# A two-layer transformer with routed experts: indirect stores, expert weights and one sequence's gathers at other places of a written-out order

## The chip, the core and the metric

The kernel runs on one core of a Trainium2 chip. The metric is the device time of one execution in microseconds (us). Engines: TensorE (PE, matrix products), VectorE (DVE), ScalarE (ACT), GpSimd (POOL) and SyncE (SP, which only issues DMAs). Each engine runs its own list of instructions in order and waits on semaphores for the others. All DMAs that SP issues stand in one queue, spread over the core's 16 DMA engines; indirect DMAs are issued from POOL and have a queue of their own.

## What is computed

Sixteen sequences of 512 tokens with 256 channels pass four blocks with residuals; each begins with a layer norm.

```
x = x + attention(norm(x))      # 16 heads of 16, rotary, window of 128 keys
x = x + experts(norm(x))        # router picks 2 of 8 experts for each token
x = x + attention(norm(x))      # 16 heads, xpos rotary, biases, full causal
x = x + norm(x) @ ternary(w).T  # weights rounded to -1, 0, 1 times a scale
```

An expert is `y = (silu(x W1a + b) * (x W1b + b)) W2 + b2` with a hidden width of 512. A token's two results are added with the softmax weights of the two experts, scaled to sum to one.

## The kernel before

The program has three phases. Phase one (tensors a0, attention and router together, from 0 to about 1100 us) and phase three (a1, attention and ternary product, from about 1807 us) are built by one function, `pipeline`. Phase two, `experts`, lies between them.

**The written-out order.** `pipeline` works in turns `i` = -2 to 17. In turn `i` several sequences are in flight, each at another stage: sequence `m = i + 2` is normed, projected to queries and keys, rotated and split into bf16 parts; sequence `s = i + 1` has its scores computed once (steps S) so that DVE finds each row's maximum; sequence `i` has its scores computed transposed (steps T), exponentiated on ACT and multiplied by the values (PV); sequence `o = i - 1` gets its output product, second norm and, in phase one, its router scores ("gates", 20 steps on DVE); the normed rows of sequence `r = i - 2` are stored by expert. `turn(i)` gives each step a number between about 0 and 1, its place in the turn. The steps are sorted by that number, and every engine takes from the sorted list those that concern it, in that order. The numbers thus set the order on each engine, not a time; semaphores do the waiting.

**The loop that passes through DRAM.** The parts of queries and keys of sequence `m` go PE (L994) -> DVE rotation (L871 in phase one, L867 in phase three) -> POOL (L526, L527 combine; L533, L537 take the parts apart, with ACT casts L601 and L604 between) -> SP stores to `a_parts_dram` (L434, nine DMAs) -> SP loads them back by head, `a_qst` and `a_kst`, one pair for each of four head groups ("stack", L444). Head group 3's pair has the place 1.0, the end of the turn. The negated row maxima (`a_nmt`, 16 KB, L449) of the sequence that is next are stored between the stacks of groups 1 and 2; the first T product (L1122) of the next turn waits for them.

**Scatters.** The eight steps ("scatter", r, k) of a turn are indirect DMAs (L507) that POOL issues: two choices of expert times four blocks of 128 tokens. Besides its rows, a scatter waits until the stack of head group 3 of the sequence `r + 3` has landed, and until ACT has done the exponentials that stand ahead of it in the order (`exps_before`).

**Expert weights.** The 24 chunks of the experts' weights (8 experts, 3 each, 128 x 1024 floats) are split in phase one into a high part and a remainder: "fetch" (SP, L408, 512 KB in), "high" (ACT, L556), "rest" (POOL, L476, the subtraction) and "keep" (SP, L413, 1024 KB out to `ws_dram`). There is one buffer: a fetch waits until the chunk before has been kept. A table, `CHUNKS`, says in which turn and where each begins: two in turn -1, one in each of turns 0 to 13, four in each of turns 14 and 15.

**Second fill.** Phase three begins by loading two rows per token from the experts' output `ys`, with indirect DMAs on POOL ("gather", L517), and DVE adds them with their weights ("mix", L725). Turns -2 and -1 fill the pipeline. DVE's mixes of a sequence wait for its gathers; sequence 1's stood in turn -2 behind all that POOL does for sequence 0's queries and keys. At the start of turn -1 stands "quantise" (DVE L680 to L695, PE L1011), the rounding of the last weights, and PE takes v of sequence 0 (L994) and its S steps behind it.

Of the kernel before, what the change touches and what calls it, by code (L numbers as in the profile page):

```python
# [26 lines left out]
NE, FF = 8, 512  # L27
# [78 lines left out]
def pipeline(nc, name, x_in, x_out, w_all, w_out, tables, biases, window, scale, consts, routed, mixed, ternary_w):  # L106
# [22 lines left out]
    def main_steps(i):  # L129

        units = [(g, b) for g in range(NG) for b in range(NT)]
        t_of = {b: [k for k, st in enumerate(t_steps) if st[0] == b] for b in range(NT)}

        def scores(u):
            return [(t_steps[k][2] * t_steps[k][4] + 256, ("T", i, u[0], k)) for k in t_of[u[1]]]

        timed = scores(units[0])
        for n, u in enumerate(units):
            nxt = scores(units[n + 1]) if n + 1 < len(units) else []
            timed += nxt[:1] + [(4 * p_width[u[1]], ("PV", i) + u)] + nxt[1:]  # L140
        total, at, out = sum(c for c, _ in timed), 0, []
        for c, st in timed:
            out.append(((at + c / 2) / total, st))
            at += c
        return out

    def turn(i):
        s, m, o = i + 1, i + 2, i - 1
        out = []
        if 0 <= i < B:  # L150
            out += [(0.05, ("minus", i, 1, 0)), (0.19, ("minus", i, 1, 1))]
            main = main_steps(i)
            out += main
            done = {st[2]: pos for pos, st in main if st[0] == "PV" and st[3] == NT - 1}
            for g in range(NG):
                out.append((done[g] + 0.001, ("sums", i, g)))
                if g < NG - 1:
                    out += [(done[g] + 0.035, ("flip", i, g)), (done[g] + 0.055, ("scale", i, g))]
        if 0 <= o < B:
            out += [(0.02, ("flip", o, NG - 1)), (0.04, ("scale", o, NG - 1)), (0.08, ("back", o, 0)),  # L160
                    (0.105, ("back", o, 1)), (0.13, ("out", o, 0)), (0.15, ("out", o, 1)), (0.155, ("add", o, 0)),
                    (0.175, ("add", o, 1))]
            out += [(0.185 + 0.015 * t, ("stats2", o, t)) for t in range(NT)] + [(0.235, ("aggr2", o))]
            if routed:
                out += [(0.28 + 0.02 * t, ("norm2", o, t)) for t in range(NT)]
                out += [(0.18, ("y", o)), (0.54, ("turn2", o, 0)), (0.56, ("turn2", o, 1)), (0.64, ("score", o)),
                        (0.789, ("exp2", o)), (0.873, ("place", o))]
                out += [(0.76 + 0.0112 * k, ("gates", o, k)) for k in range(20)]
            else:
                out += [(0.255 + 0.015 * t, ("norm2", o, t)) for t in range(NT)]  # L170
                out += [(0.355, ("turn2", o, 0)), (0.37, ("turn2", o, 1)), (0.41, ("last", o, 0)), (0.42, ("last", o, 1)),
                        (0.435, ("final", o, 0)), (0.445, ("final", o, 1)), (0.45, ("y", o))]
        if routed and 0 <= i - 2 < B:
            out += [(0.165 + 0.024 * k, ("scatter", i - 2, k)) for k in range(2 * NT)]
        if routed:
            for j, (at_turn, at) in enumerate(CHUNKS):
                if at_turn == i:
                    out += [(at, ("fetch", j)), (at + 0.14, ("high", j)), (at + 0.145, ("rest", j)), (at + 0.17, ("keep", j))]
            if i == B:
                out.append((0.03, ("pads",)))  # L180
        if 0 <= s < B:
            lo, hi = 0.03, 0.97
            out += [(lo + (hi - lo) * (k + 0.5) / NS, ("S", s, k // NSG, k % NSG)) for k in range(NS)]
            out += [(0.01, ("v", s)), (0.035, ("vcopy", s, 0)), (0.055, ("vcopy", s, 1)), (0.575 if mixed else 0.70, ("minus", s, 0, 0)), (0.68 if mixed else 0.78, ("minus", s, 0, 1))]
        for n, back in ((m, 1), (m + 1, 0)):
            if not 0 <= n < B or n == m and m and not mixed:
                continue
            if mixed:
                steps = [(0.48, ("load", n)), (1.07, ("aggr", n))]
                for t in range(NT):  # L190
                    first = 0.69 + 0.01 * t if n == 1 else 0.36 + 0.02 * t
                    steps += [(first, ("gather", n, 0, t)), (0.775 + 0.03 * t, ("mix", n, 0, t)),
                              (0.80 + 0.03 * t if n else 0.44 + 0.02 * t, ("gather", n, 1, t)), (0.92 + 0.022 * t, ("mix", n, 1, t)),
                              (1.0 + 0.015 * t, ("stats", n, t))]
            else:
                steps = [(0.55, ("load", n)), (0.88, ("aggr", n))] + [(0.80 + 0.02 * t, ("stats", n, t)) for t in range(NT)]
            out += [(at - back, st) for at, st in steps if n == 0 and back or n and int(at) == back]
        if biases and 0 <= m < B:
            out.append((0.26 if m else 0.99, ("shift", m)))
        if biases and m == 0:  # L200
# [22 lines left out]
    with ctx:  # L223
        def sb(n, shape, dt=F32):
            return ctx.enter_context(nc.sbuf_tensor(f"{name}_{n}", shape, dt))
# [32 lines left out]
        stats, stats2 = (sb(f"stats{i}", [P, NT, 6]) for i in range(2))  # L258
# [916 lines left out]
NW = KC * 2 * FF + FC * D  # L1175
WCOLS = 2 * FF


CHUNKS = [(-1, 0.25), (-1, 0.60)] + [(i, 0.13) for i in range(B - 2)] \
    + [(i, 0.02 + 0.18 * n) for i in (B - 2, B - 1) for n in range(4)]  # L1180


def turns_of_two(fori, step, count):

    step(None, Seq(None, 0))
# [378 lines left out]
```

How the kernel before makes its waits and increments, by code:

```python
        @block.sync  # L389
        def _(sp):
            if mixed:
                sp.dma_start(yrow[:, :, :], yrow_d).then_inc(index_loaded, 16)
                sp.dma_start(gate[:, :, :], gate_d).then_inc(index_loaded, 16)
            sp.dma_start(xt[0][:, :, :], x_in[0].rearrange("(t p) d -> p t d", p=P)).then_inc(x_loaded[0], 16)
            sp.dma_start(w_raw, w_all).then_inc(w_loaded, 16)
            sp.dma_start(ident[:, :], ident_d).then_inc(ident_loaded, 16)
            for dst, src in loads:
                sp.dma_start(dst, src).then_inc(const_loaded, 16)
            sp.wait_ge(ones_done, 1)
            for i in range(2):
                sp.dma_start(kst[i][ROWS:AUG, :, :], junk[0:2 * H, 0, :]).then_inc(ones_loaded, 16)
            for st in order:
                if st[0] == "fetch":
                    j = st[1]
                    e, c = divmod(j, NW // WCOLS)
                    src = w1_d[e][:, c, :] if c < KC else w2_d[e].rearrange("p c n -> p (c n)")
                    sp.wait_ge(ws_stored, 16 * j)
                    sp.dma_start(ws[:, 1, :], src).then_inc(ws_loaded, 16)
                elif st[0] == "keep":
                    j = st[1]
                    e, c = divmod(j, NW // WCOLS)
                    sp.wait_ge(rest_done, j + 1)
                    sp.dma_start(ws_d[e][:, :, c * WCOLS:(c + 1) * WCOLS], ws[:, :, :]).then_inc(ws_stored, 16)
                elif st[0] == "pads":
                    sp.wait_ge(counted_rows, 1)
```

## Time and profile before

| | us |
|---|---|
| median of three runs (2976.92 to 2982.33) | 2978.64 |
| the profiled execution, its own time | 2977.46 |
| its span, first to last instruction | 2975.8 |
| PE busy | 2530.3 (85%) |
| DVE busy | 1704.9 (57%) |
| ACT busy | 1375.7 (46%) |
| POOL busy | 922.9 (31%) |

The mean granted clock of TensorE was 0.927 of full speed. Read the busy shares as averages over three phases. The order is fixed, so a wait of one engine is handed on to all that stand behind it in the order of another. The chain of waits of the whole program says little of phase one, since it ends where the second phase's loops begin; the turns of phase one are read with sums by stretch, the waits of single turns, and the engines' instructions in order of time. A turn is counted here from one first exponential (ACT L629) of a sequence to that of the next.

### The profile page before, as it was taken

The page shows a single profiled execution, that of the slowest core. Times are in us where ns is not written, and L with a number is a line of the kernel's source. Part 1 is how long each engine was busy: PE and PEld are TensorE (multiplying, and loading weights), DVE is VectorE, ACT ScalarE, POOL GpSimd, SP SyncE. Part 2 cuts the span into 40 slices and gives each one's busy share as a digit, 9 for nine tenths or more (in the row PEclk, how much of TensorE's full clock was granted, in tenths as well). Part 3 has the DMA queues.
Part 4 walks back from the last instruction along what each step waited for, and adds up shares of the span by engine and source line. Part 5 has one row for each costly group of instructions (what it writes and reads, how often), then busy time and mean ns, then how long its engine had stood idle before and what let it go on. Part 6 is the DMA issues. An engine that isn't in the chain of part 4 may idle for free. (4 is left out here: it accounts for less than half of the span.)

```text
span 2975.8 us, 51500 instructions
## 1 busy us (share of the span) xinstructions
PE 2530.3 (85%) x17918; PEld 1733.0 (58%) x17918; DVE 1704.9 (57%) x5704; ACT 1375.7 (46%) x2419; POOL 922.9 (31%) x863
## 2 busy tenths in 40 slices
PE   3688888888888739999999993489989999999897
PEld 2355555555565428888888882245555555555554
DVE  3566666666766334444444442576667776666751
ACT  2345555555555413333333331156555655565553
POOL 3424553345435220000000003443444443344300
PEclk7799999999999759999999996699999999999998
DMA  4555556555665367767767753454344445344420
GB/s 136 182 168 166 160 160 184 172 157 155 184 174 169 139 227 250 252 239 253 260 238 251 258 206 106 127 166 126 114 120 143 134 142 145 115 114 135 122 72 15
DMA packets 261846, 493.73 MB, mean 166 GB/s; under 512 B 25608, under 2 KB 192904, under 8 KB 251656
## 3 DMA queue, kind: packets, MB, share of 16 engines
q1 hardware_dynamic: 243736, 437.07, 47.2%
q0 software_dynamic: 17904, 54.02, 5.4%
q8 instruction: 117, 1.92, 0.3%
q14 instruction: 89, 0.73, 0.1%
HBM read 301.48 MB, written 188.35 MB: 165 GB/s over the span
## 5 line engine op out<-in xcount | busy, mean ns | idle before, releaser
L629 ACT ACTIVATE a_pr<-a_bank 128x512 f32<-128x512 f32 (+1 forms) x1152 | 641.6, 573 | 559.9 <-PE a_bank L999 546.0
L887 DVE CUSTOM_DVE_ANT_0 a_junk<-a_bank,a_smask 128x256 bf16<-128x256 f32 (+3 forms) x1536 | 654.7, 464 | 405.4 <-PE a_bank L1096 404.2
L1096 PE MATMUL a_bank<-a_kst,a_qst 96*128 96x256 bf16 (+3 forms) x2048 | 452.4, 295 | 81.1 <-DVE a_nmax L887 29.1
L1122 PE MATMUL a_bank<-a_qst,a_kst 98*128 98x256 bf16 (+3 forms) x2048 | 442.6, 291 | 44.5 <-ACT a_pr L629 27.1
L1140 PE MATMUL a_bank<-a_pr,a_va 128*32 128x256 f32 (+3 forms) x4096 | 358.1, 426 | 83.0 <-ACT a_pr L629 80.0
L1401 PE MATMUL e_bank<-e_xh,e_w 128*128 128x512 f32 x1248 | 391.0, 395 | 1.4 <-DVE e_xl L1382 1.4
L1096 PEld LDWEIGHTS a_bank<-a_kst,a_qst 96*128 96x128 bf16 x2048 | 171.8, 101 | 329.9 <-DVE a_nmax L887 95.2
L999 PE MATMUL a_bank<-a_mask,a_identb 128*128 128x512 bf16 (+2 forms) x1152 | 359.8, 312 | 0.0
L1122 PEld LDWEIGHTS a_bank<-a_qst,a_kst 98*128 98x128 bf16 x2048 | 182.6, 102 | 163.6 <-ACT a_pr L629 75.0
L1401 PEld LDWEIGHTS e_bank<-e_xh,e_w 128*128 128x128 f32 x1248 | 229.6, 189 | 48.7 <-DVE e_xl L1382 1.8
L1401 PE MATMUL e_bank<-e_xl,e_w 128*128 128x512 f32 x624 | 246.5, 395 | 0.0
L1345 ACT ACTIVATE e_sa<-e_bank,e_b 128x512 f32<-128x512 f32 x156 | 107.3, 688 | 289.3 <-PE e_bank L1401 289.2
L1323 POOL DMA_DIRECT2D ys<-e_yt x39 | 29.5, 756 | 677.2 <-DVE e_yt L1363 659.8
L1374 DVE SCALAR_TENSOR_TENSOR e_gf<-e_bank,e_b,e_sa 128x512 f32<-128x512 f32 x156 | 117.2, 751 | 194.5 <-ACT e_sa L1345 194.5
L1415 PE MATMUL e_bank<-e_w,e_gh 128*128 128x256 f32 x1248 | 221.0, 278 | 2.9 <-DVE e_gl L1378 2.9
L1140 PEld LDWEIGHTS a_bank<-a_pr,a_va 128*32 128x32 f32 x4096 | 86.0, 111 | 225.0 <-issue 115.9
L507 POOL DMA_INDIRECT xs<-e_rn,e_row x128 | 127.7, 998 | 234.0 <-DMA a_kst<-a_parts_dram 127.9
L1415 PEld LDWEIGHTS e_bank<-e_w,e_gh 128*128 128x128 f32 x1248 | 192.3, 189 | 4.8 <-DVE e_gl L1378 3.4
L882 DVE TENSOR_REDUCE a_nmax<-a_bank 128x2 f32<-128x512 f32 (+1 forms) x192 | 130.1, 685 | 83.1 <-PE a_bank L999 83.1
L1415 PE MATMUL e_bank<-e_w,e_gl 128*128 128x256 f32 x624 | 173.3, 278 | 0.0
L1378 DVE TENSOR_TENSOR e_gl<-e_gf,e_gh 128x512 fp32r<-128x512 f32 x156 | 108.0, 693 | 109.8 <-ACT e_gh L1350 109.8
L1350 ACT CAST e_gh<-e_gf 128x512 fp32r<-128x512 f32 x156 | 96.9, 621 | 143.2 <-DVE e_gf L1374 143.2
(173 smaller groups left out, 4545.2 us busy)
## 6 DMA issues: line engine op xcount, KB each, us to landing
e_w<-ws_dram SPq DMA_DIRECT2D x39, 2048.0 KB, 8.8
a_parts_dram<-a_parts SPq DMA_DIRECT2D x224, 256.0 KB, 3.9
a_qst<-a_parts_dram SPq DMA_DIRECT2D x128, 384.0 KB, 7.0
a_kst<-a_parts_dram SPq DMA_DIRECT2D x128, 384.0 KB, 8.6
e_w<-ws_dram SPq DMA_DIRECT2D x39, 1024.0 KB, 6.0
a_parts_dram<-a_parts SPq DMA_DIRECT2D x32, 768.0 KB, 3.7
ws_dram<-a_ws SPq DMA_DIRECT2D x24, 1024.0 KB, 4.4
e_xg<-xs SPq DMA_DIRECT2D x39, 512.0 KB, 6.5
```

The source lines that it names most:

```text
L507: pool.indirect_dma_start(xs, bass.IndirectOffsetOnAxis(ap=row[r % 2][:, k, t:t + 1], axis=0), rn[r % 2][:, t, :], None).then_inc(scattere ...
L629: nc.scalar.activation(pr[b][:, h:h + per, :], TB_[at % 2][:, 0:per * w].rearrange("p (h w) -> p h w", h=per), ACT.Exp, scale=scale).then_ ...
L882: last = nc.vector.tensor_reduce(nmax[:, qb, g * HG + h:g * HG + h + per], SB_[at % 2][:, 0:per * w].rearrange("p (h w) -> p h w", h=per), ...
L887: last = nc.vector.tensor_tensor_reduce(junk[:, at % 2, j * w:(j + 1) * w], SB_[at % 2][:, j * w:(j + 1) * w], smask[:, T - w:T], scale=-1 ...
L999: return nc.tensor.matmul(out, identb[:, :], rhs, start=False, stop=True, skip_group_check=True)
L1096: last = nc.tensor.matmul(out[:, j * w:(j + 1) * w], q[0:ROWS, hh, qb * P:(qb + 1) * P], k[0:ROWS, hh, k0:k0 + w], start=not whole or j == ...
L1122: nc.tensor.matmul(out[:, j * w:(j + 1) * w], k[0:AUG, hh, b * P:(b + 1) * P], q[0:AUG, hh, q0:q0 + w], start=(j == 0), stop=False, skip_g ...
L1140: last = nc.tensor.matmul(PVB[32 * j:32 * (j + 1), q0:q0 + w], va[i % 2][:, b, (g * HG + j) * VW:(g * HG + j) * VW + 32], pr[b][:, j, :], ...
L1374: nc.vector.scalar_tensor_tensor(gf[f % 2][:, :], BB[f % 2][:, :], b1[s.slot][:, FC + f:FC + f + 1], sa[f % 2][:, :], ALU.add, ALU.mult).t ...
L1378: nc.vector.tensor_tensor(gl[s.slot][:, f, :], gf[f % 2][:, :], gh[s.slot][:, f, :].bitcast(F32), ALU.subtract).then_inc(gl_done, 1)
L1401: last = nc.tensor.matmul(out[:, :], first(s.slot, low)[:, kc, col:col + P], x[s.slot][:, kc, :], start=(p == 0), stop=(p == 3 * KC - 1))
L1415: last = nc.tensor.matmul(YB[n][:, (t % 2) * D:(t % 2 + 1) * D], x[s.slot][:, f, t * P:(t + 1) * P], second(s.slot, low)[:, f, :], start=( ...
```

## The change

Four edits, all but one of them numbers of the table of places.

1. The eight scatters of a turn stand at 0.135 + 0.018 k, before at 0.165 + 0.024 k.
2. The router's steps on DVE: the first fifteen gates at 0.73 to 0.877 (before 0.76 to 0.917), the last five at 0.92 to 0.968 (before 0.928 to 0.973); "exp2" at 0.757 (0.789), PE's "place" at 0.90 (0.873).
3. Chunks: two in each of turns 0 to 11, at 0.13 and 0.62; none in turns -1 and 12 to 15. The high part is still cast on ACT, the remainder is still taken on POOL.
4. Phase three, sequence 1 alone: its load, gathers, mixes and statistics stand in turn -2 among the projection steps of sequence 0, before between places 0.48 of turn -2 and 0.07 of turn -1.

```diff
-                        (0.789, ("exp2", o)), (0.873, ("place", o))]
-                out += [(0.76 + 0.0112 * k, ("gates", o, k)) for k in range(20)]
+                        (0.757, ("exp2", o)), (0.90, ("place", o))]
+                out += [(0.73 + 0.0105 * k if k < 15 else 0.92 + 0.012 * (k - 15), ("gates", o, k)) for k in range(20)]
...
-            out += [(0.165 + 0.024 * k, ("scatter", i - 2, k)) for k in range(2 * NT)]
+            out += [(0.135 + 0.018 * k, ("scatter", i - 2, k)) for k in range(2 * NT)]
...
-            for j, (at_turn, at) in enumerate(CHUNKS):
-                if at_turn == i:
-                    out += [(at, ("fetch", j)), (at + 0.14, ("high", j)), (at + 0.145, ("rest", j)), (at + 0.17, ("keep", j))]
+            for j, (fetch, high, rest, keep) in ((2 * i, (0.13, 0.27, 0.275, 0.29)), (2 * i + 1, (0.62, 0.90, 0.915, 0.93))):
+                if 0 <= j < NE * NW // WCOLS:
+                    out += [(fetch, ("fetch", j)), (high, ("high", j)), (rest, ("rest", j)), (keep, ("keep", j))]
...
-                steps = [(0.48, ("load", n)), (1.07, ("aggr", n))]
+                steps = [(0.48, ("load", n)), (1.07, ("aggr", n))] if n != 1 else [(-0.30, ("load", n)), (0.295, ("aggr", n))]
                 for t in range(NT):
-                    first = 0.69 + 0.01 * t if n == 1 else 0.36 + 0.02 * t
+                    if n == 1:
+                        steps += [(0.002 + 0.005 * t, ("gather", n, 0, t)), (0.075 + 0.01 * t, ("mix", n, 0, t)),
...
```

**POOL, one turn of the middle of phase one.** `xs<-e_rn,e_row` are scatters, `a_lean1` and its like the second norm's statistics (aggr2), `a_ws` the remainder of a chunk, `a_qk<-a_rt` the rotation of the new sequence. Before:

```order
L507 DMA xs<-e_rn,e_row 69632x256 x3
L493 TENSOR_SCALAR a_lean<-a_mv 128x4
L494 TENSOR_SCALAR a_ve<-a_mv 128x4
L496 TENSOR_TENSOR a_rstd<-a_ve,a_power 128x4
L498 TENSOR_TENSOR a_shift<-a_lean,a_rstd 128x4
L507 DMA xs<-e_rn,e_row 69632x256 x2
L476 TENSOR_TENSOR a_ws<-a_ws 128x1024
L507 DMA xs<-e_rn,e_row 69632x256 x3
L526 TENSOR_TENSOR a_qk<-a_rt 128x512
```

The same stretch now, from the end of the turn before (L481 is now the line of the remainder, L512 of the scatters):

```order
L481 TENSOR_TENSOR a_ws<-a_ws 128x1024
L512 DMA xs<-e_rn,e_row 69632x256 x6
L498 TENSOR_SCALAR a_lean<-a_mv 128x4
L499 TENSOR_SCALAR a_ve<-a_mv 128x4
L501 TENSOR_TENSOR a_rstd<-a_ve,a_power 128x4
L503 TENSOR_TENSOR a_shift<-a_lean,a_rstd 128x4
L512 DMA xs<-e_rn,e_row 69632x256 x2
L481 TENSOR_TENSOR a_ws<-a_ws 128x1024
L531 TENSOR_TENSOR a_qk<-a_rt 128x512
```

Six scatters instead of three stand ahead of the second norm's statistics, and all eight ahead of the first chunk's remainder. What stands ahead of the rotation in the turn is the same in sum; the second chunk's remainder is new and stands at the end of the turn before.

**SP, from the load of a sequence to the start of the next turn.** `a_qst` and `a_kst` of 96x2048 are the stacks of one head group, `a_qst<-a_nmt` the row maxima. Before:

```order
L426 DMA a_xt<-in_x 128x4x256
L434 DMA a_parts_dram<-a_parts 128x2x512 x6
L444 DMA a_qst<-a_parts_dram 96x2048
L444 DMA a_kst<-a_parts_dram 96x2048
L444 DMA a_qst<-a_parts_dram 96x2048
L444 DMA a_kst<-a_parts_dram 96x2048
L449 DMA a_qst<-a_nmt 2x8x512
L444 DMA a_qst<-a_parts_dram 96x2048
L444 DMA a_kst<-a_parts_dram 96x2048
L444 DMA a_qst<-a_parts_dram 96x2048
L444 DMA a_kst<-a_parts_dram 96x2048
L408 DMA a_ws<-in_we 128x1024
```

Now, the same stretch up to the stack of group 3, without its first two pairs' rows:

```order
L431 DMA a_xt<-in_x 128x4x256
L413 DMA a_ws<-in_we 128x1024
L439 DMA a_parts_dram<-a_parts 128x2x512 x6
```

```order
L454 DMA a_qst<-a_nmt 2x8x512
L449 DMA a_qst<-a_parts_dram 96x2048
L449 DMA a_kst<-a_parts_dram 96x2048
L418 DMA ws_dram<-a_ws 256x1x1024
L449 DMA a_qst<-a_parts_dram 96x2048
L449 DMA a_kst<-a_parts_dram 96x2048
L413 DMA a_ws<-in_we 128x1024
```

The second chunk's fetch (512 KB) stands ahead of the six stores, and its keep (1024 KB) ahead of head group 3's stack.

**DVE, second fill (phase three, turn -2 into -1).** `a_xt<-a_yg` are mixes; L680 and what follows is the rounding of the weights. Before:

```order
L853 TENSOR_TENSOR a_xl<-a_bank,a_xh 128x512
L867 SCALAR_TENSOR_TENSOR a_rt<-a_bank,a_bqk,a_tab 128x512 x8
L725 SCALAR_TENSOR_TENSOR a_xt<-a_yg,a_gate,a_xt 128x256 x8
L703 BN_STATS a_stats<-a_xt 128x6
L680 MEMSET a_ot 128x128
L681 TENSOR_REDUCE a_mv<-a_on 128x1
```

Now:

```order
L730 SCALAR_TENSOR_TENSOR a_xt<-a_yg,a_gate,a_xt 128x256 x4
L858 TENSOR_TENSOR a_xl<-a_bank,a_xh 128x512
L679 COPY a_ot<-a_ot 128x127 x2
L682 TENSOR_TENSOR a_boa<-a_bank,a_ot 128x256
L858 TENSOR_TENSOR a_xl<-a_bank,a_xh 128x512
L730 SCALAR_TENSOR_TENSOR a_xt<-a_yg,a_gate,a_xt 128x256 x4
L708 BN_STATS a_stats<-a_xt 128x6 x4
L714 BN_AGGR a_mv<-a_stats 128x2 x4
L872 SCALAR_TENSOR_TENSOR a_rt<-a_bank,a_bqk,a_tab 128x512 x8
L685 MEMSET a_ot 128x128
L686 TENSOR_REDUCE a_mv<-a_on 128x1
```

The eight mixes of sequence 1 stood between the rotations and the rounding; four now stand ahead of sequence 0's turning, four between its projections' inputs and its rotations.

## Rows read from the trace of the kernel before

**Rows 1.** Sums by stretch, turns of phase one: us, then busy us by engine
```profile
50.00:109.70 59.70, 28.69 (x129) 17.18 (x130) 30.23 (x148) 8.51 (x12) 19.74 (x14) 0.64 0.71 207
164.30:223.10 58.80, 52.88 (x428) 34.24 (x428) 40.40 (x198) 32.18 (x57) 19.22 (x17) 0.92 0.51 152
223.10:823.20 600.10, 523.15 (x4262) 342.22 (x4261) 397.34 (x1980) 321.88 (x561) 272.53 (x250) 0.93 0.55 168
823.20:940.80 117.60, 102.84 (x855) 67.92 (x854) 78.17 (x388) 64.26 (x113) 52.80 (x46) 0.94 0.55 167
940.80:1001.90 61.10, 50.06 (x370) 28.89 (x368) 32.93 (x180) 28.23 (x49) 18.97 (x16) 0.80 0.46 156
1001.90:1053.50 51.60, 39.20 (x291) 21.23 (x291) 11.53 (x48) 25.68 (x46) 18.98 (x16) 0.80 0.40 143
```
**Rows 2.** Instructions in order of time, PE, turn 5: start, us, [idle before]
```profile
433.24 1.08 PE L1140 MATMUL a_bank<-a_pr,a_va 128*32 128x256 f32 x8 [3.95 <-ACT a_pr L629]
...
452.82 0.18 PE L1046 MATMUL a_bank<-a_chosen,a_before 128*128 128x8 bf16 x1 [2.10 <-DVE a_chosen L783]
...
462.19 0.39 PE L1122 MATMUL a_bank<-a_qst,a_kst 98*128 98x256 bf16 x2 [0.71 <-DMA a_qst<-a_nmt]
```
**Rows 3.** Sums by stretch, the 3.4 us behind the first of these stalls
```profile
433.30:436.70 3.40, 3.40 (x26) 1.40 (x27) 2.37 (x10) 2.13 (x4) 3.34 (x3) 0.50 0.00 0
```
**Rows 4.** Instructions in order of time, POOL and DVE, turn 5
```profile
409.13 1.10 POOL L507 DMA_INDIRECT xs<-e_rn,e_row  x1 [11.13 <-DMA a_kst<-a_parts_dram]
...
424.15 1.28 DVE L871 TENSOR_TENSOR a_rt<-a_bank,a_tab 128x512 f32<-128x512 f32 x2
...
429.13 1.27 POOL L526 TENSOR_TENSOR a_qk<-a_rt 128x512 f32<-128x512 f32 x1
```
**Rows 5.** Instructions in order of time, POOL, turn 1, which has no scatters
```profile
188.31 1.29 POOL L526 TENSOR_TENSOR a_qk<-a_rt 128x512 f32<-128x512 f32 x1 [3.08 <-DVE a_rt L871]
```
**Rows 6.** DMA issues in order of time, SP, turn 5
```profile
444.97 4.22 SPq L434 DMA_DIRECT2D a_parts_dram<-a_parts  x6
...
453.77 0.42 SPq L444 DMA_DIRECT2D a_kst<-a_parts_dram  x1
```
**Rows 7.** DMA issues in order of time, SP, turn -1, which has two chunks
```profile
87.07 4.65 SPq L434 DMA_DIRECT2D a_parts_dram<-a_parts  x6
...
97.25 0.43 SPq L444 DMA_DIRECT2D a_kst<-a_parts_dram  x1
97.72 0.56 SPq L413 DMA_DIRECT2D ws_dram<-a_ws  x1
```
**Rows 8.** DMA issues by line, 97.2 to 97.9 us: KB, us from issue to landing
```profile
ws_dram<-a_ws SPq DMA_DIRECT2D x1, 1024.0 KB, 7.1
...
a_kst<-a_parts_dram SPq DMA_DIRECT2D x1, 384.0 KB, 4.9
```
**Rows 9.** Instructions in order of time, PE, end of turn -1
```profile
108.58 0.61 PE L1122 MATMUL a_bank<-a_qst,a_kst 98*128 98x256 bf16 x2 [8.44 <-DMA a_qst<-a_nmt]
```
**Rows 10.** Who waited for whom, 940.8 to 1001.9 us, turn 14: us, times, longest
```profile
PE a_bank L1140 <- ACT a_pr L629: 8.9, 3, 3.3
ACT a_ws L556 <- DMA a_ws<-in_we: 8.6, 3, 3.6
```
**Rows 11.** Who waited for whom, 1001.9 to 1053.5 us, turn 15
```profile
PE a_bank L1140 <- ACT a_pr L629: 11.2, 5, 4.3
```
**Rows 12.** Instructions in order of time, all engines, the second fill
```profile
1815.29 1.76 DVE L668 TENSOR_TENSOR a_wl<-a_rt,a_wh 128x1536 fp32r<-128x1536 f32 x1 [7.49 <-ACT a_wh L551]
1815.62 2.25 POOL L517 DMA_INDIRECT a_xn<-ys,a_yrow  x1 [0.30 <-issue]
...
1874.39 0.35 SPq L444 DMA_DIRECT2D a_qst<-a_parts_dram  x1
...
1886.76 0.59 PE L1011 MATMUL a_bank<-a_mv,a_ot 128*128 128x1 f32 x2 [36.90 <-DVE a_mv L681]
...
1891.73 0.40 PE L1096 MATMUL a_bank<-a_kst,a_qst 96*128 96x128 bf16 x4
```

More of the change, by code:

```diff
@@ L188, in turn @@
             if mixed:
-                steps = [(0.48, ("load", n)), (1.07, ("aggr", n))]
+                steps = [(0.48, ("load", n)), (1.07, ("aggr", n))] if n != 1 else [(-0.30, ("load", n)), (0.295, ("aggr", n))]
                 for t in range(NT):
-                    first = 0.69 + 0.01 * t if n == 1 else 0.36 + 0.02 * t
+                    if n == 1:
+                        steps += [(0.002 + 0.005 * t, ("gather", n, 0, t)), (0.075 + 0.01 * t, ("mix", n, 0, t)),
+                                  (0.08 + 0.01 * t, ("gather", n, 1, t)), (0.23 + 0.01 * t, ("mix", n, 1, t)),
+                                  (0.275 + 0.005 * t, ("stats", n, t))]
+                        continue
+                    first = 0.36 + 0.02 * t
                     steps += [(first, ("gather", n, 0, t)), (0.775 + 0.03 * t, ("mix", n, 0, t)),
@@ L196, in turn @@
                 steps = [(0.55, ("load", n)), (0.88, ("aggr", n))] + [(0.80 + 0.02 * t, ("stats", n, t)) for t in range(NT)]
-            out += [(at - back, st) for at, st in steps if n == 0 and back or n and int(at) == back]
+            out += [(at - back, st) for at, st in steps if n == 0 and back or n and (at >= 1) == back]
         if biases and 0 <= m < B:
@@ L1176 @@
 WCOLS = 2 * FF
-CHUNKS = [(-1, 0.25), (-1, 0.60)] + [(i, 0.13) for i in range(B - 2)] \
-    + [(i, 0.02 + 0.18 * n) for i in (B - 2, B - 1) for n in range(4)]
 def turns_of_two(fori, step, count):
```

## The prediction, made before the changed kernel had run

> **What bounds the kernel now.** The sums by stretch come first [rows 1]: from turn 2 on a turn of phase one takes 60.0 us (600.1 for ten), PE is busy for 52.3 of them, DVE 39.7, ACT 32.2, POOL 27.3, and the DMA engines 55%. Turn 1, which has no scatters yet, takes 58.8. So PE leads, but 7.7 us of a turn it stands still. PE's instructions in order of time show where [rows 2]: 3.95 us for an exponential, 2.10 for the router's choice on DVE, 0.71 for the landing of the row maxima at the first T product of the next turn. The 3.4 us behind such a stall are at the lower clock level, 1.2 GHz instead of 2.4 [rows 3], so each stall costs some 1.7 us more.
>
> It would be wrong to add all this up as gain, because the last of the three waits ends a loop through DRAM that is as long as the turn. From the first exponential of turn 5 (402.7) the loop runs: rotation inputs ready on DVE 425.4, that is 22.7 us later; POOL begins the rotation at 429.1, 3.7 us late, since scatters and a chunk's remainder are ahead of it [rows 4]; six stores from 445.0, 15.8 us later; the pair of stacks at 453.8 [rows 6], 8.8 later; first T product at 462.2 [rows 2], 8.4 later. 22.7 + 3.7 + 15.8 + 8.8 + 8.4 = 59.4, and 0.65 to the exponential is 60.1, the turn. PE waits only 0.71 us at the end because its own stalls fill the time. What is taken from PE's stalls alone comes back as a longer wait at L1122. I read the change by this loop.
>
> **Turns 2 to 11: scatters, gates and a second chunk.**
> - The scatters begin when the stack of head group 3 has landed, at 409.1 [rows 4]. From there to the rotation POOL spends 20.0 us, some of it waiting for exponentials between scatters. At the closer places all eight need only T steps that are done by then, so this wait goes; work of about 15 us is left (eight issues of 1.1 with 0.2 to 0.3 between, 2.5 for the statistics, 2.4 for the remainder), and the rotation could start at once when its inputs are there: 3.7 us gained, no more.
> - The second chunk's keep now stands ahead of head group 3's stack. In turn -1 a keep stood so: a stack landed at 97.25 + 4.9 = 102.2, the keep behind it at 97.72 + 7.1 = 104.8 [rows 7, 8]. It takes 2.6 us of the queue, and the scatters begin so much later, at about 411.7: with 15 us of work the rotation would start at 426.8, 1.4 late instead of 3.7. So 2.3 gained.
> - The second fetch stands ahead of the six stores. Turn -1 again shows it: first store to the stack of keys took 97.25 - 87.07 = 10.2 us there [rows 7], 8.8 in turn 5 [rows 6]. 1.4 lost.
> - PE's stalls at L1140 and L1046 shrink or go (place is later by 0.027, the choice earlier by 0.034 of a turn, 3.7 us together, against a wait of 2.10), but the loop ends when it ends, so PE waits some 5 us at L1122 instead, and what follows runs at the lower clock. This lengthens the beginning of the loop: in turn 1, which begins so, the inputs come at 188.3 [rows 5], 24.0 us after its exponential at 164.3 [rows 1], against 22.7: 1.3 lost.
> - Second "high" on ACT and "rest" on POOL (2.4 us): ACT waits for PE at the end of a turn, POOL is idle there. Nothing, as long as the remainder is done before the queue has worked off the stacks of groups 0 to 2. Should it not be, its 2.4 us delay the scatters too.
>
> Sum: -2.3 + 1.4 + 1.3 = +0.4; with rounding I take 0 per turn, 0 for ten. Bounds per turn: -3.7 (no loss from the DMAs) to +4.0 (keep and fetch both in full on the loop, 2.6 + 1.4), that is -37 to +40.
>
> **Turns 0 and 1**: the fetch's 1.4 each, nothing to gain: +2.8. **Turns 12 and 13** lose their one chunk: now 117.6 for two [rows 1]; without remainder and with early scatters they follow turn 1: -1.8.
>
> **Turn -1** loses two chunks. At its end PE waits 8.44 us for the row maxima until 108.58 [rows 9]. Fetch and keep are in the queue ahead of them: 1.4 and 2.6 as above, and about 0.3 for what the first chunk's remainder costs POOL. -4.3; bounds 0 and -8.4, the whole wait.
>
> **Turns 14 and 15** lose eight chunks, and here lies most of the gain, since no loop through DRAM is left (no new sequence is projected). Turn 14 takes 61.1 us with fewer products than the turns before; the clock is at 0.80 of full, against 0.93 [rows 1]. ACT stands three times for a fetch, 8.6 us, and PE for its exponentials 8.9 [rows 10]; in turn 15 PE stands 11.2 [rows 11]. With four chunks through one buffer, each cast waits for its load. Turn 14: of PE's 8.9 some 3 stay, because the second norm waits for POOL's six scatters ahead of its statistics; 5.9 go, with 1.6 at L1046. A clock of 0.80 means 40% of the time at the lower level: 24 us, in which 12 are lost; I give back 7.5, since a stall or two remain. -15.0; bounds -8.6 (ACT's own waits alone) and -22. Turn 15: 11.2 less the same 3 is 8.2; its 20 us at the lower level lose 10, of which I give back 5: -13; bounds -7 and -20. Behind turn 15 nothing is gained or lost: padding the expert regions begins when its gates are done and needs its time.
>
> **Second fill of phase three.** PE stands 36.9 us, to 1886.76, for the rounding on DVE, which stands behind sequence 1's mixes; v takes until 1891.73, where the S steps begin [rows 12]. In the new order the rounding follows the rotations directly, and v is long done. The next to end is then the stack of sequence 0: issued at 1874.39 [rows 12], its key half takes 4.9 us where nothing crowds it [rows 8], so 1879.3 to 1879.7. That is -12.2. Sequence 0's own path: DVE and POOL wait for each other and for gathers there, so four gathers and four mixes before its norm are hidden; I take 0.2 lost. **A rule that speaks against this:** one gather took 2.25 us, twice the 1.1 of a scatter's issue [rows 4, 12], while DVE ran the 1.76 us of L668 beside it [rows 12]. The Trainium skill (SBUF — State Buffer, section "SBUF: two separate sides") says that GpSimd can't write a DMA's descriptors while VectorE holds the port pair both share. By it the moved gathers, now beside DVE's mixes, could each take up to 1.1 us longer, four of them ahead of sequence 0's statistics: the fill would give -8 instead of -12. L668 moves six times as many elements as a mix, so I expect less. Bounds: -6 and -14.
>
> **Sum.** 0 + 2.8 - 1.8 - 4.3 - 15.0 - 13.0 - 12.0 = -43.3. Against the profiled execution's own time (2977.5; its span is 1.7 shorter) 2934.2; the median lies 1.2 above that execution: 2935.4, I say 2936.
>
> **Rivals.**
> - *The loop doesn't bind.* If the maxima come early once stores and stacks are issued earlier, each of turns 2 to 13 gets the 3.7 us: another -40, 2895. For it: POOL, which starts the loop, gets freer. Against: turn 1, with the rotation on time, is only 1.2 shorter and ends in the same DMA wait.
> - *The queue binds (the other side).* Keep, fetch and stacks of a turn share one queue; if the keep lengthens the loop too, by a later start of POOL, and the six scatters ahead of the second norm hold ACT and so the T products, a turn grows by 2.6 + 1.4 + 1.4 = 5.4, twelve turns by 65: 2936 + 65 = 3001. It decides from 3.6 us per turn on. For it: DMA is busy 55% and crowded just there. Against: the keep stands behind the maxima in the queue.
> - *The last turns give back little.* With exponentials and T products taking turns on two banks, the stalls of turns 14 and 15 stay in other places, and the clock low: only the 8.6 and 7 of the fetch waits go, 12 less gain: 2948.
> - *Nothing in sum.* Turns grow by 3 to 4 us and eat the rest: 2977.
>
> **How the numbers follow.** My forecast 0.60, its own range 2920 to 2951; the last turns give back little 0.17; the loop doesn't bind 0.09; the queue binds 0.10 (0.08 of it slower); nothing in sum 0.04. A measurement of this kernel tells 0.2%, 6 us, from no change. Slower 0.08, same 0.04, faster 0.88. The range, 2908 to 2962, takes in the two inner cases and half of each outer one.
>
> **What would show it.** Right: turns 2 to 11 at 59 to 61.5 us, POOL's rotation no longer 3.7 us late, the wait at L1046 gone, and instead 3 to 7 us of PE at the first T product for the row maxima; the scatters beginning about 2.6 us later after that product's turn start; turn 14 at 44 to 49 us and turn 15 at 36 to 41, with a clock above 0.85; the first T product of turn 0 near 104; S steps of the second fill from about 1880 less the gain before. Wrong: turns 2 to 11 beyond 62 or under 58, ACT waiting at the second norm for 5 us and more, or a second fill whose first S product waits for DVE again.

## The result, and where the time went

The changed kernel takes 2932.82 us (median of four runs; one of them, at 3707.74 us, was disturbed and is left out of the ratio). The kernel before, run with it, takes 2980.48. The ratio is 0.9834, 95% interval 0.9814 to 0.9855: by the ratio 49 us less, where 43 were forecast. The profiled execution took 2926.71 us, its span is 2925.0 at a mean granted clock of 0.943 (0.927 before). The line numbers of the engines' parts of `pipeline` are larger by five in the changed kernel: L629 is now L634, L1122 is L1127.

The sums by stretch of the changed kernel, which answer to [rows 1] (turn -1, turn 1, turns 2 to 11, 12 and 13, 14, 15):

```profile
50.00:104.40 54.40, 28.15 (x128) 17.02 (x130) 30.22 (x148) 6.91 (x11) 15.12 (x12) 0.66 0.62 169
161.70:221.40 59.70, 51.49 (x422) 33.89 (x428) 41.49 (x198) 32.81 (x58) 21.56 (x18) 0.95 0.56 176
221.40:822.00 600.60, 510.10 (x4192) 337.04 (x4261) 412.72 (x1980) 327.73 (x571) 295.85 (x260) 0.96 0.62 194
822.00:936.30 114.30, 101.51 (x840) 66.90 (x853) 79.08 (x388) 61.60 (x110) 48.00 (x44) 0.97 0.50 152
936.30:982.30 46.00, 40.49 (x364) 24.67 (x368) 31.53 (x175) 24.15 (x45) 9.56 (x12) 0.96 0.19 58
982.30:1023.60 41.30, 33.93 (x286) 18.95 (x291) 12.99 (x60) 21.68 (x42) 9.53 (x12) 0.92 0.11 39
```

The ten steady turns together did not move (600.1 to 600.6 us), although POOL has 23 us more to do in them. Turn 14 lost 15.1 us, turn 15 10.3, and the clock of both rose from 0.80 to 0.96 and 0.92.

PE's waits in the ten turns tell how that zero came about. First the kernel before (223.1 to 823.2 us), then the changed one (221.4 to 822.0); columns: who waited for whom, us in total, times, longest:

```profile
PE a_bank L1140 <- ACT a_pr L629: 39.7, 10, 4.0
PE a_bank L1046 <- DVE a_chosen L783: 21.1, 10, 2.1
...
PE a_bank L1122 <- DMA a_qst<-a_nmt: 2.2, 3, 0.8
```
```profile
PE a_bank L1127 <- DMA a_qst<-a_nmt: 28.5, 10, 4.7
PE a_bank L1101 <- DVE a_nmax L892: 21.2, 28, 1.0
PE a_bank L1153 <- ACT a_nmt L625: 10.3, 10, 1.1
...
PE a_bank L1145 <- ACT a_pr L634: 7.4, 13, 1.0
```

The two big stalls, 61 us in ten turns, are gone but for 7.4 us in pieces of 1.0 at most. In their place PE waits 28.5 us for the row maxima at the first T product, 21 for DVE's maxima in short pieces, 10 for the copy of the maxima.

The larger of the two old stalls, at the exponentials, had not begun with PE. In turn 5 of the kernel before, ACT stood for POOL's rotation ahead of the exponentials that PE waited for until 433.24 [rows 2]:

```profile
431.65 1.05 ACT L601 CAST a_parts<-a_qk 128x1024 bf16<-128x1024 f32 x1 [6.90 <-POOL a_qk L527]
432.60 1.08 ACT L629 ACTIVATE a_pr<-a_bank 128x512 f32<-128x512 f32 x2
```

POOL's late rotation thus stands behind this stall as well as in the loop through the stores. In the ten turns ACT waited 69.1 us for it before and 36.8 us in the changed kernel.

Turn 5 of the changed kernel, engine by engine:

```profile
408.66 1.10 POOL L512 DMA_INDIRECT xs<-e_rn,e_row  x1 [12.77 <-DMA a_kst<-a_parts_dram]
...
423.38 1.29 POOL L531 TENSOR_TENSOR a_qk<-a_rt 128x512 f32<-128x512 f32 x1
```
```profile
421.53 1.28 DVE L876 TENSOR_TENSOR a_rt<-a_bank,a_tab 128x512 f32<-128x512 f32 x2
```
```profile
439.55 4.27 SPq L439 DMA_DIRECT2D a_parts_dram<-a_parts  x6
...
450.04 0.42 SPq L449 DMA_DIRECT2D a_kst<-a_parts_dram  x1
...
451.45 0.67 SPq L454 DMA_DIRECT2D a_qst<-a_nmt  x1
```
```profile
458.15 0.39 PE L1127 MATMUL a_bank<-a_qst,a_kst 98*128 98x256 bf16 x2 [1.96 <-DMA a_qst<-a_nmt]
```

The turn began at 400.12. POOL now begins the rotation 23.3 us into it, 0.6 us behind DVE's last input (422.8); in [rows 4] it was 26.4 and 3.7 us late. From there to the stores it takes 16.2 us (15.8 before). From the stores to the stack of keys it takes 10.5 where [rows 6] had 8.8.

**The second fill.** PE's first S product of phase three, which came behind DVE's rounding in [rows 12]:

```profile
1848.82 0.61 PE L1101 MATMUL a_bank<-a_kst,a_qst 96*128 96x128 bf16 x4 [18.96 <-DMA a_kst<-a_parts_dram]
```

It comes 71.8 us after DVE's first instruction of the phase (1777.05); before, 84.4 (1807.32 to 1891.73). It waits for the stack, no longer for DVE.

### The profile page after: what moved, and what is told of

It reads as the page before. It is cut to its first block and busy times, and to the rows that moved or that the text cites. A ratio compares the mean times of both kernels' runs of the same rounds, so it can differ in the third digit from the quotient of the medians.

```text
span 2925.0 us, 51326 instructions
## 1 busy us (share of the span) xinstructions
PE 2492.1 (85%) x17745; PEld 1718.6 (59%) x17918; DVE 1723.0 (59%) x5704; ACT 1369.4 (47%) x2419; POOL 923.2 (32%) x863
## 5 line engine op out<-in xcount | busy, mean ns | idle before, releaser
L634 ACT ACTIVATE a_pr<-a_bank 128x512 f32<-128x512 f32 (+1 forms) x1152 | 638.0, 573 | 552.5 <-PE a_bank L1004 302.3
L1127 PE MATMUL a_bank<-a_qst,a_kst 98*128 98x256 bf16 (+3 forms) x2048 | 434.6, 286 | 72.9 <-DMA a_qst<-a_nmt 43.4
L1145 PE MATMUL a_bank<-a_pr,a_va 128*32 128x256 f32 (+3 forms) x4096 | 350.2, 418 | 35.5 <-ACT a_pr L634 33.8
L1127 PEld LDWEIGHTS a_bank<-a_qst,a_kst 98*128 98x128 bf16 x2048 | 178.3, 99 | 189.9 <-ACT a_pr L634 78.4
L1004 PE MATMUL a_bank<-a_mask,a_identb 128*128 128x128 bf16 (+2 forms) x979 | 283.3, 289 | 0.0
L512 POOL DMA_INDIRECT xs<-e_rn,e_row x128 | 127.7, 998 | 299.7 <-DMA a_kst<-a_parts_dram 138.2
```

The costliest lines, as they stand in the source:

```text
L512: pool.indirect_dma_start(xs, bass.IndirectOffsetOnAxis(ap=row[r % 2][:, k, t:t + 1], axis=0), rn[r % 2][:, t, :], None).then_inc(scattere ...
L634: nc.scalar.activation(pr[b][:, h:h + per, :], TB_[at % 2][:, 0:per * w].rearrange("p (h w) -> p h w", h=per), ACT.Exp, scale=scale).then_ ...
L1004: return nc.tensor.matmul(out, identb[:, :], rhs, start=False, stop=True, skip_group_check=True)
L1127: nc.tensor.matmul(out[:, j * w:(j + 1) * w], k[0:AUG, hh, b * P:(b + 1) * P], q[0:AUG, hh, q0:q0 + w], start=(j == 0), stop=False, skip_g ...
L1145: last = nc.tensor.matmul(PVB[32 * j:32 * (j + 1), q0:q0 + w], va[i % 2][:, b, (g * HG + j) * VW:(g * HG + j) * VW + 32], pr[b][:, j, :], ...
```

## The experiments

Two theories were to be told apart. **The loop**: a turn of phase one is as long as the way rotation - stores - stack - row maxima - first T product, and what PE's stalls give up comes back as a wait there. **The rivals**: PE's stalls bind, so the turn shrinks with them; or the queue binds, so it grows with every DMA put ahead. The table holds means over turns 2 to 11 of each kernel's one profile, in us after a turn's first exponential, worked out from the starts of the instructions in each trace.

```
                       first    rotation  six     stack    first T   next
                       scatter  on POOL   stores  of keys  product   turn
before                   6.5     26.4     42.7    50.5     59.4      60.0
changed                  8.8     24.0     40.4    50.6     59.3      60.1
chunks alone             8.4     26.7     43.2    52.7     61.6      62.2
scatters, gates alone    6.9     23.4     40.2    48.4     57.3      58.0
changed, fetch early     8.6     24.1     41.2    49.4     58.5      59.2
changed, keep behind     7.2     23.6     40.3    50.4     59.0      59.8
before, maxima first     7.1     26.4     42.8    50.7     58.9      59.5
changed, maxima first   11.1     25.9     43.4    53.6     59.8      60.5
 + keep behind           8.9     23.8     40.2    50.3     56.0      56.7
 + scatters' wait        6.6     22.8     39.4    49.6     55.4      56.1
```

How far one profile can be trusted shows where two kernels have the same order in these turns: the ten took 600.1 and 601.7 us (before; the fill alone), 600.6 and 604.2 (changed; with the late scatters of experiment 5), 560.9 and 572.6 (the last kernels of experiments 4 and 6). A difference under 0.4 us a turn is not shown by such a pair, and one of 1.2 came up once without a cause in the order.

**1. The three parts, each alone on the kernel before.** First the chunks, edit 3 of the change:

```diff
-            for j, (at_turn, at) in enumerate(CHUNKS):
+            for j, (fetch, high, rest, keep) in ((2 * i, (0.13, 0.27, 0.275, 0.29)), (2 * i + 1, (0.62, 0.90, 0.915, 0.93))):
```

> The kernel before with the chunks alone moved (two a turn in turns 0 to 11, none in -1 and 12 to 15). Scatters, gates and the second fill stay as they were. Loop theory: in turns 2 to 11 the keep delays the scatters by 2.6 us and the fetch the stores by 1.4, and nothing is won back, since the scatters keep their far places: up to +4.0 us a turn, so 62 to 64 us instead of 60.0. Against that turn -1 gives back some 5, turn 14 some 15, turn 15 some 10 us. Sum: +40 + 3 - 30 = about +10 us, 2988. Rival (the wider spacing hides the chunk, turns stay at 60): -30 us, 2950. Rival (the queue binds, 5.4 a turn): 3005.

2969.42 us, ratio 0.9973 (0.9961 to 0.9984). The turns 2 to 11 grew by 22.3 us, 2.2 each, and turns 14 and 15 lost 16.0 and 11.7. The direction in each place is the theory's; the cost per turn is half of the 4.0 that was the bound, so the sum has the other sign than expected.

Then the fill, edit 4:

```diff
-                steps = [(0.48, ("load", n)), (1.07, ("aggr", n))]
+                steps = [(0.48, ("load", n)), (1.07, ("aggr", n))] if n != 1 else [(-0.30, ("load", n)), (0.295, ("aggr", n))]
```

> The kernel before with the second fill alone changed. Theory A: all of the difference behind phase three's start belongs to this edit: 12.6 us until the first score product, some 4 in the rest of turn -1 and some 4.5 in the turns of phase three, so -21 us, 2959. Theory B: the 4 and the 4.5 are not this edit's but scatter of the execution: -12.6, 2968. Phase one and two unchanged within 1 us in both.

2963.59 us, ratio 0.9946 (0.9928 to 0.9964): -16 us, between the two. By the trace: first S product 13.2 us sooner (71.2 us after DVE's start against 84.4), from there to the first T product 45.4 against 48.2. All four profiles without this edit have 48.2 to 48.5, the ten with it 44.2 to 46.8. So 1.4 to 4 us in the rest of turn -1 are this edit's. A gain in the turns of phase three is not shown: they take 998.3 to 1002.6 us without the edit (1002.6 in the profile of before) and 996.6 to 1002.5 with it.

Last the scatters and gates, edits 1 and 2:

```diff
-            out += [(0.165 + 0.024 * k, ("scatter", i - 2, k)) for k in range(2 * NT)]
+            out += [(0.135 + 0.018 * k, ("scatter", i - 2, k)) for k in range(2 * NT)]
```

> The kernel before with scatters, gates, exp2 and place at the new places, chunks and fill as before. Loop theory: POOL begins the rotation on time (3.7 us earlier a turn), the turn's start runs slower by 1.3, so -2.4 us a turn in turns 2 to 13, about 57.7 instead of 60.0, -29 us in all, 2950; PE then waits for the row maxima instead of exponentials and the router's choice. Rival (PE's stalls bind, no loop): their 7.7 us a turn go, 52 to 54 us a turn, -75. Rival (POOL's delay did not matter): 60 us a turn, 2979.

2952.20 us, ratio 0.9918 (0.9886 to 0.9949). Turns 2 to 11 take 580.0 us, 2.0 less each, where the loop gave 2.4 and the rivals 7.7 or nothing. PE's stalls of 61 us went here too (4.2 are left), and 20 us came of it. The three parts' gains, 8.0 + 16.1 + 24.4 = 48.5 us by their ratios, make up the 49.5 of the whole, and in the ten turns +22.3 - 20.1 = +2.2 stands beside the +0.5 measured, which two profiles can't tell apart.

**2. The loop cut.** The row maxima of head half 0 stand in the order, and so in SP's queue, behind the stacks of groups 0 and 1. They were taken ahead of them, on SP alone:

```diff
-            for st in order:
+            ahead = [("minus", s, 0, 1) for s in range(B - 1)] if routed else []
+            for st in [early for st in order if st not in ahead
+                       for early in ([("minus", st[1] - 1, 0, 1)] if routed and st[0] == "stack" and st[1] and st[2] == 0 else []) + [st]]:
```

> The changed kernel, phase one alone edited: SP issues the row maxima's DMA (16 KB) of head half 0 ahead of the stacks of groups 0 and 1 instead of behind them. They are on the SBUF side ready at 442.3 in turn 5 and SP is free at 443.9, yet they are issued at 451.45. Loop theory: the first T product no longer waits for the loop (2.9 us a turn by the waits' sum); next is the stack of group 0, landed at 455, before PE's own work ends at 456.3. So -2 to -2.8 us a turn in 11 to 13 turns: -22 to -35 us, 2898 to 2911. Rival (another wait takes its place at once, such as the first S product for its stack, or DVE): 0 to -8 us. Slower would be a surprise.

2917.81 us, ratio 0.9802 (0.9782 to 0.9821), 9 us less than the changed kernel by the ratios, and the ten turns did not gain: 604.6 us. The wait for the maxima is gone from PE's list, the gain lies in turns -1 and 0 (the first exponential of turn 1 is at 148.8 instead of 161.7). The turn was bound by a second loop, which this profile shows, SP and POOL:

```profile
384.55 0.62 SPq L420 DMA_DIRECT2D ws_dram<-a_ws  x1
385.22 0.59 SPq L451 DMA_DIRECT2D a_qst<-a_parts_dram  x1
385.85 0.47 SPq L451 DMA_DIRECT2D a_kst<-a_parts_dram  x1
```
```profile
398.04 1.10 POOL L514 DMA_INDIRECT xs<-e_rn,e_row  x1 [13.51 <-DMA a_kst<-a_parts_dram]
```

The stack of head group 3, with the keep's 1024 KB just ahead, is issued at 385.85 in turn 4, and the first scatter, which waits for it, starts 12.2 us later; behind the scatters come the rotation (14.7 us), the six stores (17.4), the stack of keys (10.4), and again the stack of group 3 (5.8): 60.5 us, as long as the mean of the ten turns.

The same edit on the kernel before:

> The kernel before with the maxima's DMA alone ahead of the stacks of groups 0 and 1. PE waited only some 0.7 us a turn there. Theory (PE's own stalls at the exponentials and the router's choice, 6 us a turn, bind as long as the loop does): turns 2 to 11 gain no more than 1 us each, 59 to 60; turn -1 and turn 0 give 8 to 12 us as in the changed kernel; 2960 to 2970. Rival (the loop alone bound, the stalls only filled its time): turns 2 to 11 fall to 56 or 57, 2930 to 2940.

2955.87 us, ratio 0.9928 (0.9912 to 0.9945). The ten turns take 595.4 us, 0.5 less each, hardly more than two profiles differ by, and PE waits there as before:

```profile
PE a_bank L1142 <- ACT a_pr L631: 39.6, 10, 4.0
PE a_bank L1048 <- DVE a_chosen L785: 21.0, 10, 2.1
```

Of the 21 us gained, 10.0 lie ahead of turn 0 and 5.6 in turns 0 and 1. So in the kernel before two things were about equally long, the loop and PE's own work with its stalls. With the loop cut the stalls hold the turn (0.5 gained at most), and the larger of them is POOL's late rotation, for which ACT waits 69.1 us here too; with the stalls gone and POOL on time the loop holds it (2.0 gained, experiment 1).

**3. The terms of the queue, each alone on the changed kernel.** The second chunk's keep behind the stack of group 3:

```diff
-(2 * i + 1, (0.62, 0.90, 0.915, 0.93)))
+(2 * i + 1, (0.62, 0.90, 0.915, 1.001)))
```

> The changed kernel with only the second chunk's keep moved behind the stack of group 3. It measures the term of 2.6 us: scatters begin 8.5 us after a turn's first exponential now, and should begin 5 to 6 after it. Loop theory: the rotation begins up to 2 us earlier if its inputs are there, and the maxima's loop gets shorter by that: -0.5 to -2 us a turn in 11 turns, 2910 to 2925. Rival (the keep was free where it stood): 0, 2930. A loss of 1 to 2 us a turn if the fetch behind the keep now holds up the output and the second half of the maxima.

2930.79 us, ratio 0.9853 (0.9832 to 0.9874), no difference that can be told. The scatters begin 1.6 us earlier, the rotation only 0.3, since then it waits for its inputs; the turn shrinks by 0.3, which one profile doesn't show.

The second fetch at 0.31 instead of 0.62, out of the stores' way:

> The changed kernel with the second chunk's fetch alone moved from 0.62, ahead of the six stores, to 0.31, behind the first chunk's keep, where SP has nothing to do. It measures the term of 1.4 us. Theory (the fetch lengthens the maxima's loop): stores land 1.4 us earlier, turns 0 to 11 shorter by 0.7 to 1.4 us, 2916 to 2925. Rival (the fetch was free, or SP now waits for the keep's landing in front of the stores): 2930 or more, turns 2 to 11 at 60 us.

2925.29 us, ratio 0.9841 (0.9815 to 0.9866), which does not tell it from the changed kernel; the trace does. From the stores to the stack of keys it is 8.2 us instead of 10.2, but the stores are 0.8 later; the ten turns take 591.8 us, 0.9 less each, and PE's wait for the maxima falls from 28.5 to 10.3 us. As the queue stands here, the fetch is the larger of the two costs.

**4. Both loops cut.** Maxima first, and the keep at 1.001:

> The kernel with the maxima first, and the second chunk's keep at place 1.001, behind the stack of head group 3, instead of 0.93. Theory (two loops): with the maxima out of the way a second loop of 60.6 us bound the turn: in turn 5 of that kernel stack of group 3 issued 385.85, landed 398.04 (12.2 us, the keep's 1024 KB ahead of it), rotation 412.76 (14.7), stores 430.14 (17.4), stack of group 0 at 440.57 (10.4), the next at 446.41 (5.8). Without the keep ahead the stack of group 3 should land in some 7 us: the turn falls to 56 to 57.5 us, -3 to -4 in 11 to 12 turns: 2918 less 33 to 48, 2870 to 2885. Rival (the scatters, not the stack, are late): turns stay at 59 to 60, 2905 to 2918.

2880.73 us, ratio 0.9682 (0.9663 to 0.9701). The keep, worth 0.3 us a turn or nothing by itself, is worth 3.8 here: 566.5 us for ten turns against 604.6. Then, with these, the scatters wait for the stack of group 2:

```diff
-                        pool.wait_ge(stack_loaded[(r + 3) % 2][NG - 1], 32 * ((r + 3) // 2 + 1))
+                        pool.wait_ge(stack_loaded[(r + 3) % 2][NG - 2], 32 * ((r + 3) // 2 + 1))
```

> Maxima first, keep behind, and the scatters wait for the stack of head group 2 instead of 3. Theory: POOL starts the scatters some 5 us earlier, so the loop through stack 3, scatters and rotation is cut; then PE's own work and its short stalls bound the turn, 54.5 to 56.5 us, 2855 to 2875. Rival (scatters beside the stack slow both, or DVE and PE bind already): no more than 5 us below the kernel without this edit.

**2872.16 us, ratio 0.9642 (0.9623 to 0.9660): the best of all, 107 us below the kernel before and 57 below the changed one by the ratios.** Ten turns take 560.9 us:

```profile
208.10:769.00 560.90, 506.69 (x4263) 334.13 (x4262) 414.12 (x1980) 327.98 (x571) 295.93 (x260) 0.97 0.67 207
```

PE is busy for 50.7 of 56.1 us, and its list of waits holds no DMA.

**5. The last turns.** In the changed kernel PE still stood 3.18 us in turn 14 and 3.93 in turn 15, each for exponentials, while ACT waited for the second norm's statistics behind six scatters on POOL. First the changed kernel (936.3 to 1023.6 us), then the one of this experiment (940.2 to 1020.3):

```profile
ACT e_rn L583 <- POOL a_shift L503: 7.2, 2, 3.9
```
```profile
ACT e_rn L583 <- POOL a_shift L503: 2.9, 2, 1.9
```

The edit:

```diff
-            out += [(0.135 + 0.018 * k, ("scatter", i - 2, k)) for k in range(2 * NT)]
+            out += [((0.24 if i in (B - 2, B - 1) else 0.135) + 0.018 * k, ("scatter", i - 2, k)) for k in range(2 * NT)]
```

> The changed kernel with the scatters of turns 14 and 15 alone at 0.24 + 0.018 k, behind the second norm's statistics on POOL. It tests what is left of PE's stall there: 3.18 us at 951.38 and 3.93 at 996.79, each with a stretch at the lower clock. Theory (ACT's second norm waits for POOL's scatters): both gaps go, turn 14 from 46.0 to 42 to 43.5, turn 15 from 41.3 to 37 to 39, 2920 to 2926 in all. Rival (the scatters are late elsewhere and hold rn or the pads): turn 16 and what is behind it grows by the same, 2930.

2927.92 us, ratio 0.9837 (0.9820 to 0.9853); the total can't tell it, the two turns do:

```profile
940.20:983.60 43.40, 39.48 (x370) 24.16 (x368) 31.61 (x175) 24.09 (x46) 9.53 (x12) 1.00 0.21 63
983.60:1020.30 36.70, 32.21 (x291) 18.25 (x291) 12.94 (x58) 21.29 (x42) 9.53 (x12) 1.00 0.13 44
```

2.6 and 4.6 us less, and the granted clock 1.00 throughout. Nothing behind turn 15 got longer: from its end to DVE's first instruction of phase three it is 753.4 us in both.

**6. All together, which failed.** To the best kernel both the early fetch and the late scatters were added:

> All five together: maxima first, keep behind the stack of group 3, scatters waiting for group 2's stack, scatters of turns 14 and 15 behind the second norm's statistics, fetch at 0.31. If the last two add to the 2872 of the first three: turns 14 and 15 give 7 us; the fetch gives nothing once no loop binds (turns 2 to 11 stay at 56). 2863 to 2867. Rival (the loop through the stores still binds): turns at 55, 2850 to 2855.

2876.46 us, ratio 0.9667 (0.9651 to 0.9683), which doesn't tell it from the best kernel: not better. Then only the late scatters were added:

> Four of the five: maxima first, keep behind the stack of group 3, scatters waiting for group 2's stack, scatters of turns 14 and 15 late; the fetch back at 0.62. In the kernel with all five, turns 14 and 15 took 49.9 and 43.1 us, against 43.4 and 36.7 where the late scatters were tried alone, though the five kernels have the same order there. If the early fetch is what costs (by whatever it does to what lies before), turns 14 and 15 come to 43.4 and 36.7 here, 2863 to 2867. Rival (the late scatters cost once the turns before are shorter, or these two turns scatter from build to build): 47 to 50 and 41 to 43 again, 2873 to 2879.

2886.81 us, ratio 0.9689 (0.9665 to 0.9713), five runs from 2875.72 to 2894.49, slower than the best kernel. In both kernels turn 14 takes 49.9 and turn 15 43.1 us, instead of 43.4 and 36.7 (46.0 and 41.0 in the best kernel), so the fetch is not what costs. These two turns are only a part of what the last kernel lost: its ten turns take 572.6 us, against 560.9 and, with the early fetch, 560.3, though the late scatters change nothing there. Its profile is of the slowest of its five runs. Both have a wait like this in turn 15, here of the four edits:

```profile
971.48 0.90 PE L1155 MATMUL a_bank<-a_ident,a_ou 128*128 128x128 f32 x3 [4.40 <-ACT a_ou L645]
```

where in the kernel of experiment 5 the same step follows within a microsecond. The order of the instructions on ACT and DVE in these two turns is the same in all three kernels, and against experiment 5 both fall back in the same two short stretches, by about 6 us each: from 20 to 26 us into turn 14 and from 63 to 67. ACT stands at its copy (L645) 2.29 us for an event the profile doesn't name. Some of PE's records are missing there, so what PE did in the 4.4 us can't be read. **The cause is open.**

## Why the prediction was right, and where it was off

The time (2936 against 2932.8, range 2908 to 2962) and the account behind it held. Term by term, forecast and measured in us, by the first exponentials of the two profiles:

| | forecast | measured |
|---|---|---|
| turn -1 | -4.3 | -5.3 |
| turns 0, 1 | +2.8 | +3.6 |
| turns 2 to 11 | 0 | +0.5 |
| turns 12, 13 | -1.8 | -3.3 |
| turn 14 | -15.0 | -15.1 |
| turn 15 | -13.0 | -10.3 |
| fill, to the first S product | -12.0 | -12.6 |
| rest of phase three's turn -1 | none | -4.0 |
| turns of phase three | none | -4.5 |

The rows that were forecast add up to -42.5 against -43.3. The 8.5 us in the last two rows were not forecast.

- **Turns 2 to 11.** Right by the loop: the rival "the loop doesn't bind" gave -40, "the queue binds" +65. The stalls at L1140 and L1046 went and PE waits 2.9 us a turn at L1127 instead, a little under the 3 to 7 expected. Inside the zero the terms were off and cancelled, so the exact zero is in part luck. The rotation is 2.4 us earlier in the turn; the forecast had 2.3 less the clock's 1.3, which is 1.0. The 1.3 is real, but only in some turns: rotation inputs come 24.0 or 24.1 us after the first exponential in six of the ten, at a granted clock of 0.93, and 22.7 in four (turn 5 among them), at 1.00, as in all ten before; the mean is 0.8 later. Turns 4 and 5 up to that point:

```profile
340.60:364.60 24.00, 22.93 (x165) 14.87 (x166) 15.15 (x67) 16.07 (x29) 12.04 (x13) 0.93 0.52 173
400.10:422.80 22.70, 21.50 (x165) 14.18 (x166) 15.10 (x67) 15.80 (x29) 11.44 (x13) 1.00 0.56 190
```

  POOL is behind its inputs by 0.4 on average (3.7 before), where 1.4 was forecast. Against these gains the stretch from stores to stack grew by 2.4 (7.8 to 10.2), not by 1.4. Turn -1, from which the 1.4 was taken, didn't show the size of it; that a steady turn is more crowded would explain it, but was not tested.
- **Turns 12 and 13.** The forecast's -1.8 follows from no row: two turns like turn 1 take the 117.6 us that they took before. They gave 3.3, and the granted clock there rose from 0.94 to 0.97.
- **The keep's 2.6 us.** The scatters begin 2.3 us later, about as forecast, but this costs the turn 0.3 at most (experiment 3): the rotation waits for its inputs anyway. It becomes the bound once the maxima are out of the way (experiment 4).
- **Turn 14** was right in its terms: PE's wait for exponentials fell from 8.9 to 3.2 us. **Turn 15** was the mis-sized term: the wait fell from 11.2 only to 5.6, and the clock rose to 0.92, where turn 14 reached 0.96. Of the 3 us that were to stay, 3.93 stayed at one place. Experiment 5 shows what they cost with the clock that goes with them: 4.6 us.
- **Second fill.** Right in mechanism and size: S waits for the stack of sequence 0, its key half issued at 1843.44. The rule that would have given -8 did not come into play, as the issues of the gathers show, the eight moved ones and the four first of sequence 0 (ns, min/median/max):

```profile
L522 POOL DMA_INDIRECT a_yg<-ys,a_yrow x12: 940/946/1093, 1780.2 to 1808.1; - x12
```

  No gather beside a mix takes longer than a scatter (1.1 us). The Trainium skill (SBUF — State Buffer, section "SBUF: two separate sides") names VectorE operations in a two-port mode, and those with two SBUF inputs against a GpSimd operation that reads SBUF; a mix has two such inputs, and none of the twelve issues was slowed here. The section's sentence on descriptors, from which the prediction took its rule, speaks of VectorE operations in the two-port mode and not of two inputs. The one issue beside the subtraction with two such inputs (L668, now L673) took 2.30 us again (2.25 before), so the row that the rival rested on repeats; whether the subtraction is its cause was not tested.
- **Not forecast:** 1.4 to 4 us in the rest of phase three's turn -1 belong to the fill (experiment 1). I had stopped my account at the first S product. The 4.5 us of the turns behind it are not shown to be an effect of the change: profiles without the fill edit differ by 4.3 among themselves.
- **The rival "last turns give back little"** is refuted: clock 0.96 and 0.92.

## What to carry to other kernels

When a stall of the leading engine goes and the turn stays as it is, look for the loop that closes over the queue, add up its pieces from one turn to the next, and ask which entry in the queue could stand earlier than it does: here 16 KB stood behind two stacks it did not need. Cutting one loop may show nothing by itself: the first cut gave the ten turns nothing, the second 0.3 us a turn at most alone and 3.8 with the first. Before a stall is called the engine's own, follow who held it up: here one late step on POOL was both the stall and a piece of the loop. A time taken from another turn (1.4 us for the fetch) was too small for the steady one (2.4), and one turn read by itself would have hidden what the clock did in six of ten.

## What the hardware did that was not expected

The rounding of the last weights on DVE now runs beside POOL's part and rotation steps, and became up to 4.7 times as slow. Three instructions of the changed kernel, with POOL's beside them:

```profile
1824.93 2.14 POOL L542 TENSOR_TENSOR a_parts<-a_qk,a_parts 128x1024 bf16<-128x1024 f32 x1 [1.16 <-ACT a_parts L609]
1825.07 2.28 DVE L693 TENSOR_SCALAR a_on<-a_on,a_mv 128x512 f32<-128x512 f32 x1
1827.03 1.47 POOL L531 TENSOR_TENSOR a_qk<-a_rt 128x512 f32<-128x512 f32 x1
1827.39 1.39 DVE L696 TENSOR_SCALAR a_on<-a_on 128x512 f32<-128x512 f32 x1
1828.45 1.47 POOL L532 TENSOR_TENSOR a_qk<-a_rt 128x512 f32<-128x512 f32 x1
1828.82 1.39 DVE L698 TENSOR_SCALAR a_on<-a_on 128x512 f32<-128x512 f32 x1
```

Before, L693 and L696 (there L688 and L691) took 0.48 and 0.43 us with POOL idle. Each of the three now ends 0.28 to 0.29 us behind the end of the POOL instruction that was running when it began, and POOL's rotation takes 1.47 instead of 1.27. The fill alone on the kernel before shows the same durations (2.28 and 1.39). The Trainium skill (the same section) says that the port pair is an exclusive lock, which the first to start holds for its whole instruction; these rows agree. DVE's delay cost nothing, since PE waits for the stack until 18 us later. POOL's did: its two rotations, 0.4 us longer together, stand ahead of that very stack, since ACT's next cast waits for the second:

```profile
1829.95 1.04 ACT L606 CAST a_parts<-a_qk 128x1024 bf16<-128x1024 f32 x1 [5.10 <-POOL a_qk L532]
```
